# One megakernel, new queues: the output norm's sums of squares on ScalarE, setup work off VectorE, one silu for two more chunks

## The chip, the cores and the metric

One core of one Trainium2 chip runs the whole program in one launch. The metric is the device time of that launch in microseconds.

## The reference

Two layers, each a recurrent mixer followed by a mixture of experts, on an input of 16 x 16 x 8 positions with 64 channels (fp32):

```python
# mixer, both layers; H, W, B, D = 16, 16, 8, 64
feat = ln(x) @ in_w + in_b            # 64 -> 192
inp, og, fg = split(feat, 3)
inp, og, lam = silu(inp), sigmoid(og), sigmoid(fg)
# outer product by head (2x2), scans forward and back along H and along W
inp_o = (1 - lam)[..., None] * inp[..., None, :]
state = bidir_scan_h(inp_o, lam) + bidir_scan_w(inp_o, lam)
out = einsum('...hde,...hd->...he', state, og).reshape(H, W, B, D)
out = (out - out.mean(-1)) * rsqrt(out.var(-1) + 1e-5) * gamma + beta
x = x + out @ out_w + out_b
# layer 0 experts: 16, hidden 128, top 2, softmax over the two
h = silu(ln(x) @ w1[e]) * (ln(x) @ w2[e]);  x = x + sum_e gate_e * (h @ w3[e])
# layer 1 experts: 8, hidden 256, top 2
h = gelu(ln(x) @ W1[e] + b1[e]);            x = x + sum_e gate_e * (h @ W2[e] + b2[e])
```

Both feed-forward parts compute every expert for every position and weigh the results by gates that are zero outside the top two.

## The kernel before, in words

The batch is cut into four groups of two images (512 positions). A **unit** is one layer of one group: units 0 to 3 are layer 0, units 4 to 7 are layer 1. The mixer works in **chunks**: chunks 0 and 1 are the two images of unit 0 (256 positions each), chunks 2 to 8 are units 1 to 7. An expert of one unit is a **step**: steps 0 to 63 are layer 0, steps 64 to 95 layer 1; two steps make a **pair**, whose products down are weighed and added together.

Nothing is looped: the table `ORDER` lists by hand, for each engine, the stages in the order in which it runs them, and `BANK_USES` lists who uses which of the eight PSUM banks in turn. Every engine works strictly through its list; a stage that waits holds back all that is listed behind it. Stages are linked by semaphores.

One chunk of the mixer goes, with the names of the lists (number = chunk): `a_stats` (VectorE, mean and variance of the rows, and `a_parts`, `a_norm`: the norm, split into two parts), `a_turn` (TensorE transposes), `a_z` (ScalarE copy), `p_f`, `p_i`, `p_o` (TensorE, projections with `in_hi` and `in_lo`), `t_f`, `t_i`, `t_o` (ScalarE, tanh and silu), `lam_fw/rw/fh/rh` (ScalarE, decay factors), `add_w` (VectorE), `add_h` (ScalarE), `fwd_*`, `rev_*` (VectorE scans), `sum_*`, `gate_o` (VectorE), `heads` (TensorE, with `heads_w`: the first half of each result is the head sum, the second the output product), `b_stats` (statistics of the first half), `b_rstd` (GpSimd), `b_res` (VectorE, residual), `e_stats`, `e_norm`, `e_parts`, `e_turn`, `e_z` (second norm, transposed into `tok_z`).

The experts: `up_a`, `up_b` (TensorE, two matmuls each), `act` (ScalarE, silu, layer 0; gelu in layer 1), `hid` (VectorE product, layer 0) or `act_b` (ScalarE gelu of the second half, layer 1), `down` (TensorE), `weigh` (VectorE), `add` (GpSimd). The gates: `logits` (TensorE), `top` (VectorE), `t_m` (ScalarE), `gates` (GpSimd), `g_turn` (TensorE), `g_copy` (ScalarE), then a write to DRAM and a broadcast back by SyncE's queue into `gates_b`. `x_turn` and `x_res` add the experts' sum to the rows; layer 1 of a group needs them.

Expert weights of layer 0 are split into two parts as well: `round` (ScalarE) makes the high part of a pair, `split` (GpSimd) the low part, and `up_a` of the pair waits for it. Pairs 0 and 1 wait for the first block of up weights, pairs 2 to 7 for the second.

Setup before: VectorE rounds and subtracts the gate weights (`gate_w0`), spreads the input weights over both parities and splits them (`in_w`), and widens the biases and vectors (`b_wide0`, `v_wide0`), which TensorE turns (`b_turn0`, `v_turn0`). Small products (`products0`) and their copies (`biases0`) give folded biases.

For chunks in `BY_TANH` the silu of `t_i` is made of a tanh and an Identity on ScalarE and one more product on VectorE (`value`); for the others it is one Silu:

```python
if not two_branches(c):
    nc.scalar.activation(bank, bank, ACT.Silu, bias=column(l, I_B)).then_inc(s_value, 1)
    return
```

The output norm before reads mean and variance on VectorE:

```python
for t in range(count):
    last = nc.vector.bn_stats(stats[n][:, k, t, :], ...)
link(last)
for t in range(count):
    last = nc.vector.bn_aggr(moments[n][:, k, t, :], stats[n][:, k, t, :])
```

Of the kernel before, what the change touches and what calls it, by code (L numbers as in the profile page):

```python
# [1410 lines left out]
```

## Time and profile before

| | |
|---|---|
| median of 3 runs | 256.01 us (255.82 to 257.69) |
| profiled execution | 255.79 us |
| span of its instructions | 253.9 us |
| PE busy | 210.3 us, 83% |
| DVE busy | 195.0 us, 77% |
| ACT busy | 165.8 us, 65% |
| POOL busy | 129.9 us, 51% |

The profiled execution is 1.9 us longer than its span. PE is TensorE, DVE is VectorE, ACT is ScalarE, POOL is GpSimd. Shares are averages over stages that differ: the first 51 us hold the setup and the first chunks of the mixer, then experts and mixer chunks of both layers are interleaved. A duration in the rows is that of one instruction from start to end; instructions of one engine overlap, so the distance between starts is what one costs in a row of many.

### The profile page before, as it was taken

To read this page: it belongs to the slowest core of one execution; us is meant where nothing else is said; L and a number is where in the kernel's file an instruction comes from. 1 tells how busy PE (TensorE), PEld (TensorE's weight loads), DVE (VectorE), ACT (ScalarE), POOL (GpSimd) and SP (SyncE) were. 2 spreads that over 40 slices of the span, in tenths; PEclk is the share of its full clock that TensorE was granted. 3 is DMA by queue.
4 is the path that set the end of the run, shared out by engine and by line. 5 is a ranking of instruction groups with operands and counts; after the bars stand their busy time and mean duration, and the time that the engine had idled before them with its cause. 6 is when DMAs were issued, how large, how long until landed. Compare 5 with 4: busy or idle time off the path is not lost. (4 is left out here: it accounts for less than half of the span.)

```text
span 253.9 us, 3842 instructions
## 1 busy us (share of the span) xinstructions
PE 210.3 (83%) x940; PEld 127.1 (50%) x940; DVE 195.0 (77%) x621; ACT 165.8 (65%) x323; POOL 129.9 (51%) x206
## 2 busy tenths in 40 slices
PE   0052985777979899999798999899999999999992
PEld 0042764543535555656364655555565654744640
DVE  0378499989989999959699999979996199634233
ACT  2039589948644473869578443599959998485560
POOL 3115389850875495875344541785728632453212
PEclk9999999799999999999999999999999999999998
DMA  1199700026940194009629300000800704400450
GB/s 37 53 211 185 134 1 1 0 82 137 202 83 0 44 209 88 0 8 218 114 66 203 69 0 3 1 3 3 165 1 5 167 0 108 83 0 1 88 121 21
DMA packets 18544, 18.50 MB, mean 73 GB/s; under 512 B 5350, under 2 KB 12284, under 8 KB 18524
## 3 DMA queue, kind: packets, MB, share of 16 engines
q1 hardware_dynamic: 18524, 18.28, 35.3%
q8 instruction: 7, 0.11, 0.2%
q14 instruction: 13, 0.11, 0.2%
HBM read 17.56 MB, written 0.72 MB: 72 GB/s over the span
## 5 line engine op out<-in xcount | busy, mean ns | idle before, releaser
L1232 PE MATMUL SPARE<-tok_z,up_hi 128*128 128x512 f32 x192 | 81.3, 424 | 5.0 <-ACT silu_h L837 1.6
L1233 PE MATMUL SPARE<-tok_z,up_lo 128*128 128x512 f32 x192 | 75.4, 393 | 0.0
L538 POOL TENSOR_TENSOR total<-total,weighted 128x512 f32<-128x512 f32 x39 | 50.1, 1285 | 45.2 <-DVE weighted L1158 25.9
L1350 PE MATMUL SPARE<-hidden,down 128*64 128x512 f32 x256 | 60.9, 602 | 2.3 <-DVE hidden L1137 1.2
L837 ACT ACTIVATE silu_h<-SPARE 128x512 f32<-128x512 f32 x64 | 37.8, 597 | 28.6 <-PE SPARE L1233 28.6
L1232 PEld LDWEIGHTS SPARE<-tok_z,up_hi 128*128 128x128 f32 x192 | 36.0, 188 | 34.0 <-issue 10.9
L1137 DVE TENSOR_TENSOR hidden<-silu_h,SPARE 128x512 f32<-128x512 f32 x64 | 42.0, 674 | 1.5 <-PE SPARE L1233 0.9
L1233 PEld LDWEIGHTS SPARE<-tok_z,up_lo 128*128 128x128 f32 x192 | 36.2, 188 | 5.3
L1350 PEld LDWEIGHTS SPARE<-hidden,down 128*64 128x64 f32 x256 | 16.6, 136 | 30.3 <-issue 23.7
L843 ACT ACTIVATE hidden<-SPARE,expert_bias 128x512 f32<-128x512 f32 x32 | 21.8, 683 | 10.5 <-PE SPARE L1350 9.9
L1236 PE MATMUL SPARE<-ident,parts_a 128*128 128x128 f32 x32 | 7.0, 352 | 20.5 <-DVE parts_a L1012 15.4
L850 ACT ACTIVATE hidden<-SPARE,expert_bias 128x512 f32<-128x512 f32 x32 | 21.9, 684 | 2.4 <-PE SPARE L1233 2.4
L1158 DVE TENSOR_TENSOR weighted<-SPARE,gates_b 128x512 f32<-128x512 f32 x28 | 18.6, 681 | 2.5 <-DMA gates_b<-gates_dram 1.2
L681 POOL TENSOR_TENSOR up_lo<-up_raw,up_hi 128x512 fp32r<-128x512 f32 x12 | 15.2, 1277 | 9.1 <-ACT up_hi L731 9.1
L1232 PE MATMUL SPARE<-conv_z,in_hi 128*128 128x512 f32 (+1 forms) x27 | 14.0, 520 | 4.2 <-issue 3.0
L1236 PEld LDWEIGHTS SPARE<-ident,parts_a 128*128 128x128 f32 x32 | 4.8, 179 | 22.3 <-issue 20.4
L1160 DVE SCALAR_TENSOR_TENSOR weighted<-SPARE,expert_bias,gates_b 128x512 f32<-128x512 f32 x12 | 9.0, 746 | 8.0 <-PE SPARE L1350 8.0
L757 ACT ACTIVATE conv_z<-SPARE 128x512 fp32r<-128x512 f32 (+1 forms) x9 | 4.8, 538 | 14.5 <-PE SPARE L1236 14.5
L661 POOL TENSOR_SCALAR spread_a<-moments_a 128x4 f32<-128x4 f32 (+1 forms) x9 | 2.3, 252 | 21.9 <-DVE moments_a L992 21.7
L1286 PE MATMUL SPARE<-heads_w,gated 128*128 128x128 f32 x64 | 10.1, 302 | 3.4 <-issue 2.9
L1233 PE MATMUL SPARE<-conv_z,in_lo 128*128 128x512 f32 (+1 forms) x27 | 12.7, 471 | 0.0
L741 ACT ACTIVATE norm_e<-rows,shift_e,rstd_e 128x64 f32<-128x64 f32 x28 | 10.1, 437 | 3.7 <-POOL shift_e L666 3.6
(133 smaller groups left out, 366.4 us busy)
## 6 DMA issues: line engine op xcount, KB each, us to landing
gates_b<-gates_dram SPq DMA_DIRECT2D x6, 1024.0 KB, 9.9
gates_b<-gates_dram SPq DMA_DIRECT2D x8, 512.0 KB, 6.0
up_raw<-in_L_ffn_w_dram SPq DMA_DIRECT2D x4, 384.0 KB, 7.9
gates_b<-gates_dram SPq DMA_DIRECT2D x2, 768.0 KB, 11.3
up_raw<-in_L_ffn_W_dram SPq DMA_DIRECT2D x2, 512.0 KB, 6.0
up_raw<-in_L_ffn_w_dram SPq DMA_DIRECT2D x4, 128.0 KB, 3.7
down<-in_L_ffn_w_dram SPq DMA_DIRECT2D x1, 512.0 KB, 10.4
down<-in_L_ffn_W_dram SPq DMA_DIRECT2D x1, 512.0 KB, 5.1
```

Source lines behind the costliest of these rows:

```text
L538: nc_engine.tensor_tensor(t, t, weighted[:, q % WEIGHED_RING, :], ALU.add).then_inc(s_sum, 1)
L681: nc.gpsimd.tensor_tensor(up_lo[l][:, e, :, :], up_raw[:, e, :, :], up_hi[l][:, e, :, :].bitcast(fp32), ALU.subtract).then_inc(s_split, 1)
L741: last = nc.scalar.activation(norm[n][:, k, t, :], tile[:, t // HALF, t % HALF, :], ACT.Identity, bias=shift[n][:, k, t:t + 1], scale=rstd ...
L837: nc.scalar.activation(silu_h[:, at % SILU_RING, :], spare("up_a", n), ACT.Silu).then_inc(s_silu_h, 1)
L843: nc.scalar.activation(hidden[:, hidden_slot(n) % RING, :], spare("up_a", n), ACT.Gelu, bias=expert_bias[:, 2 * i:2 * i + 1]).then_inc(s_h ...
L850: nc.scalar.activation(hidden[:, hidden_slot(n, 1) % RING, :], spare("up_b", n), ACT.Gelu, bias=expert_bias[:, 2 * i + 1:2 * i + 2]).then_ ...
L1137: nc.vector.tensor_tensor(hidden[:, hidden_slot(n) % RING, :], silu_h[:, STEP_AT[n] % SILU_RING, :], spare("up_b", n), ALU.mult).then_inc( ...
L1158: nc.vector.tensor_tensor(dst, spare("down", q), g, ALU.mult).then_inc(s_pm, 1)
L1232: nc.tensor.matmul(dst, hi, z, start=True, stop=False)
L1233: return nc.tensor.matmul(dst, lo, z, start=False, stop=True)
L1236: return nc.tensor.transpose(dst, src, ident[0:k, 0:k])
L1350: last = nc.tensor.matmul(spare("down", q)[k * D:(k + 1) * D, :], w, hidden[:, at, :], start=(j == 0), stop=(j == chunks - 1))
```

## The change

**Output norm.** The head matrix `heads_w` gets -1/64 added, so that the first half of the `heads` result is the head sum less its mean. `b_stats` moves from VectorE (4 BN_STATS and 4 BN_AGGR per chunk of four tiles) to ScalarE: one Square per tile with an accumulated sum, written in place in PSUM. GpSimd makes the variance from the sums in the same number of instructions as before.

**Setup.** `gate_w0` leaves VectorE: ScalarE rounds (`gate_hi0`), GpSimd subtracts (`gate_w0`). The input weights are rounded by ScalarE in six activations (`in_hi`) and subtracted by VectorE in six instructions (`in_w`), without `in_wide`. `b_wide0` and `v_wide0` move to ScalarE.

**Silu.** `BY_TANH` shrinks from chunks 5 to 8 to chunks 7 and 8: chunks 5 and 6 lose the tanh on ScalarE and the product on VectorE.

**Orders.** All lists of `ORDER` and `BANK_USES` are new. A path by which GpSimd could make hidden products is added, but `BY_POOL` is empty, so that none of it runs.

```diff
-BY_TANH = tuple(c for c in range(len(CHUNKS)) if UNITS_AT[CHUNKS[c][0]] not in ((0, 0), (0, 1), (0, 2), (0, 3)))
+BY_TANH = (7, 8)
+
+BY_POOL = ()
...
-        "gate_w0 a_stats0 a_stats1 in_w0 a_parts0 b_wide0 v_wide0 b_cols0 a_parts1 add_w0 a_stats2 a_stats3 "
+        "a_stats0 a_stats1 a_parts0 a_parts1 in_w0 b_cols0 v_cols0 add_w0 out_w0 fwd_w0 fwd_h0 rev_w0 rev_h0 "
...
-                nc.gpsimd.tensor_copy(heads_w[:, l, 0, :], over_d[:, :]).then_inc(s_over, 1)
+                nc.gpsimd.tensor_scalar(heads_w[:, l, 0, :], over_d[:, :], -1.0 / D, None, ALU.add).then_inc(s_over, 1)
...
+                if n == "b":
+                    link(nc.gpsimd.tensor_scalar(spread[n][:, k, t], squares[:, k, t], 1.0 / D, eps, ALU.mult, ALU.add))
...
+            def in_high(l):
+                act.wait_ge(s_in[l], 32)
+                for parity in range(2):
+                    for which in (FORGET, OUTPUT, INPUT):
+                        last = copy(of_parity(in_hi[:, l, which, :], which, parity), in_part(l, which))
+                last.then_inc(s_in_hi, 1)
...
+            def head_squares(c):
+
+                act.wait_ge(s_heads, c + 1)
+                if c >= 2:
+                    act.wait_ge(s_rstd["b"], c - 1)
+                heads = heads_of(c)[0]
+                for t in range(chunk_tiles(c)):
+                    last = nc.scalar.activation(heads[:, t, :], heads[:, t, :], ACT.Square,
+                                                accum_out=squares[:, c % 2, t:t + 1])
+                last.then_inc(s_stats["b"], 1)
...
-                link(last)
-                link(nc.vector.tensor_copy(in_hi[:, l, :, :], fog[:, :, :]))
-                nc.vector.tensor_tensor(in_lo[:, l, :, :], fog[:, :, :], in_hi[:, l, :, :].bitcast(fp32),
-                                        ALU.subtract).then_inc(s_conv_w, 1)
+                dve.wait_ge(s_in_hi, l + 1)
+                for parity in range(2):
+                    for which in (FORGET, OUTPUT, INPUT):
+                        last = nc.vector.tensor_tensor(
+                            of_parity(in_lo[:, l, which, :], which, parity), in_part(l, which),
+                            of_parity(in_hi[:, l, which, :].bitcast(fp32), which, parity), ALU.subtract)
+                last.then_inc(s_conv_w, 1)
```

**VectorE at the start of the program, before.** `stats_a` and `norm_a` belong to the first norm, `gate_parts` to the gate weights:

```order
L970 CAST gate_parts<-gate_raw 128x16 [waits conv_weights_loaded0]
L970 CAST gate_parts<-gate_raw 128x8 [waits conv_weights_loaded1]
L974 TENSOR_TENSOR gate_parts<-gate_raw,gate_parts 128x16 [waits vector_chain]
L974 TENSOR_TENSOR gate_parts<-gate_raw,gate_parts 128x8
L988 BN_STATS stats_a<-rows 128x6 [waits rows_loaded_first]
L988 BN_STATS stats_a<-rows 128x6
L992 BN_AGGR moments_a<-stats_a 128x2 [waits vector_chain]
```

**VectorE at the start, now:**

```order
L1071 BN_STATS stats_a<-rows 128x6 [waits rows_loaded_first]
L1071 BN_STATS stats_a<-rows 128x6
L1074 BN_AGGR moments_a<-stats_a 128x2 [waits vector_chain]
L1074 BN_AGGR moments_a<-stats_a 128x2
L1081 TENSOR_TENSOR norm_a<-rows,moments_a 128x128 [waits moments_ready_a]
L1071 BN_STATS stats_a<-rows 128x6 [waits rows_loaded_first]
L1071 BN_STATS stats_a<-rows 128x6
L1074 BN_AGGR moments_a<-stats_a 128x2 [waits vector_chain]
L1074 BN_AGGR moments_a<-stats_a 128x2
```

The four instructions on the gate weights, which wait for the loads of both layers' small weights, no longer stand ahead of the first statistics of the rows.

**ScalarE at the start of the program, before.** `conv_z` is `a_z`; `tanh_f` is `t_f`:

```order
L854 ACTIVATE warm<-minus_half 128x4 [waits constants_ready]
L757 ACTIVATE conv_z<-SPARE 128x256 [waits norm_turned_a]
L766 ACTIVATE tanh_f<-SPARE,half_bias 128x256 [waits columns_ready,forget_projected]
L774 ACTIVATE SPARE<-SPARE,columns 128x256 [waits input_projected]
L787 ACTIVATE tanh_o<-SPARE,half_bias 128x256 [waits output_projected]
L801 ACTIVATE lam_rh<-tanh_f 128x15x16 [waits pads_zeroed,tanh_f_ready]
L801 ACTIVATE lam_fh<-tanh_f 128x15x16 [waits pads_zeroed,tanh_f_ready]
```

**ScalarE at the start, now:**

```order
L963 ACTIVATE warm<-minus_half 128x4 [waits constants_ready]
L785 ACTIVATE in_hi<-in_raw 128x64 [waits in_weights_loaded0]
L785 ACTIVATE in_hi<-in_raw 128x64
L785 ACTIVATE in_hi<-in_raw 128x32x2
L785 ACTIVATE in_hi<-in_raw 128x64 x2
L785 ACTIVATE in_hi<-in_raw 128x32x2
L785 ACTIVATE wide<-vectors 2x64 [waits in_biases_loaded]
L785 ACTIVATE wide<-vectors 2x64
L785 ACTIVATE wide<-vectors 2x32x2
L785 ACTIVATE wide<-vectors 2x64 x2
L785 ACTIVATE wide<-vectors 2x32x2
L848 ACTIVATE conv_z<-SPARE 128x256 [waits norm_turned_a]
```

Twelve small activations on the input weights and biases now stand ahead of the first `conv_z`.

**ScalarE around the last steps of layer 0 and the first of layer 1, before** (silu_h is `act` of layer 0, line 843 and 850 are `act` and `act_b` of layer 1; `tanh_f`, `lam_*`, `tanh_i` here are chunk 7):

```order
L766 ACTIVATE tanh_f<-SPARE,half_bias 128x512 [waits lambdas_ready_rw,lambdas_ready_fw,lambdas_ready_fh,row_inputs_ready,lambdas_ready_rh,columns_ready,forget_projected]
L837 ACTIVATE silu_h<-SPARE 128x512 [waits hidden_ready0,up_first_bank]
L801 ACTIVATE lam_rw<-tanh_f 128x32x15 [waits row_scans_done,pads_zeroed,tanh_f_ready]
L801 ACTIVATE lam_rh<-tanh_f 128x2x15x16 [waits column_scans_done,pads_zeroed,tanh_f_ready]
L801 ACTIVATE lam_fw<-tanh_f 128x32x15 [waits row_scan_forward_done,pads_zeroed,tanh_f_ready]
L822 ACTIVATE tanh_m<-margin 128x4 [waits gates_ready,margin_ready]
L801 ACTIVATE lam_fh<-tanh_f 128x2x15x16 [waits column_scan_forward_done,pads_zeroed,tanh_f_ready]
L837 ACTIVATE silu_h<-SPARE 128x512 [waits hidden_ready0,up_first_bank] x2
L778 ACTIVATE tanh_i<-SPARE,half_bias 128x512 [waits input_products_ready,input_projected]
L781 ACTIVATE SPARE<-SPARE,columns 128x512 [waits tanh_i_ready]
L829 ACTIVATE gates_t<-SPARE 8x512 [waits gates_sent1,gates_turned]
L843 ACT_TABLE_LOAD [waits pair_down_done,biases_ready]
```

**The same place now** (lines 945 and 959 are the gelus):

```order
L945 ACT_TABLE_LOAD [waits pair_down_done,biases_ready]
L945 ACTIVATE hidden<-SPARE,expert_bias 128x512 [waits up_first_bank]
L959 ACTIVATE hidden<-SPARE,expert_bias 128x512 [waits up_second_bank,pair_down_done]
L945 ACTIVATE hidden<-SPARE,expert_bias 128x512 [waits pair_down_done,up_first_bank]
L959 ACTIVATE hidden<-SPARE,expert_bias 128x512 [waits up_second_bank,pair_down_done]
L917 ACTIVATE tok_z<-SPARE 128x512 [waits logits_product,up_second_bank,norm_turned_e]
L945 ACTIVATE hidden<-SPARE,expert_bias 128x512 [waits pair_down_done,up_first_bank]
L959 ACTIVATE hidden<-SPARE,expert_bias 128x512 [waits up_second_bank,pair_down_done]
L945 ACTIVATE hidden<-SPARE,expert_bias 128x512 [waits pair_down_done,up_first_bank]
L857 ACTIVATE tanh_f<-SPARE,half_bias 128x512 [waits lambdas_ready_rw,lambdas_ready_fw,lambdas_ready_fh,row_inputs_ready,lambdas_ready_rh,columns_ready,forget_projected]
L869 ACTIVATE tanh_i<-SPARE,half_bias 128x512 [waits input_projected]
L872 ACTIVATE SPARE<-SPARE,columns 128x512 [waits tanh_i_ready]
```

Chunk 7's `t_f` and `t_i` (and its `lam_*` behind them) now stand behind the first seven gelus of layer 1, where they stood ahead of them.

## Rows read from the trace of the kernel before

**Rows 1.** Busy time by stretch (windows: start:end, length, busy and count of each engine).

```profile
11.00:31.20 20.20, 10.45 (x43) 8.54 (x43) 14.80 (x69) 11.68 (x31) 8.25 (x15) 1.00 0.98 181
31.20:54.20 23.00, 17.07 (x61) 12.70 (x60) 21.38 (x85) 19.66 (x37) 19.53 (x29) 0.93 0.01 2
54.20:173.90 119.70, 109.25 (x490) 64.72 (x491) 110.46 (x312) 75.00 (x145) 66.42 (x93) 1.00 0.39 81
173.90:248.30 74.40, 72.94 (x345) 40.70 (x343) 45.58 (x152) 57.98 (x109) 32.53 (x52) 1.00 0.30 63
```

**Rows 2.** Timeline, the last 10 us (start, duration, engine, line, operation, count, idle before).

```profile
244.63 3.65 PE L1350 MATMUL SPARE<-hidden,down 128*64 128x512 f32 x16
244.93 0.75 DVE L1160 SCALAR_TENSOR_TENSOR total<-SPARE,expert_bias,gates_b 128x512 f32<-128x512 f32 x1 [5.39 <-DMA gates_b<-gates_dram]
```

**Rows 3.** Waits from 54.2 to 173.9 us (who waited for whom: us, times, longest).

```profile
ACT silu_h L837 <- PE SPARE L1233: 27.8, 35, 3.4
```

**Rows 4.** Timeline of VectorE, the first steps.

```profile
10.66 0.17 DVE L970 CAST gate_parts<-gate_raw 128x8 fp32r<-128x8 f32 x1 [1.80 <-DMA gate_raw<-in_L_ffn_Wg_dram]
...
11.03 0.34 DVE L988 BATCH_NORM_STATS2 stats_a<-rows 128x6 f32<-128x64 f32 x2
...
12.77 0.19 DVE L929 COPY in_wide<-in_raw 128x64 f32<-128x64 f32 x1
...
14.96 0.29 DVE L1012 TENSOR_TENSOR parts_a<-norm_a,parts_a 128x128 f32<-128x128 f32 x1
...
18.60 0.60 DVE L988 BATCH_NORM_STATS2 stats_a<-rows 128x6 f32<-128x64 f32 x4
```

**Rows 5.** Timeline of TensorE: first projection, the first experts.

```profile
16.53 0.58 PE L1232 MATMUL SPARE<-conv_z,in_hi 128*128 128x256 f32 x1
...
32.16 0.63 PE L1232 MATMUL SPARE<-conv_z,in_hi 128*128 128x512 f32 x1
32.59 0.63 PE L1233 MATMUL SPARE<-conv_z,in_lo 128*128 128x512 f32 x1
...
51.10 0.47 PE L1232 MATMUL SPARE<-tok_z,up_hi 128*128 128x512 f32 x1 [0.52 <-issue]
...
52.56 0.40 PE L1232 MATMUL SPARE<-tok_z,up_hi 128*128 128x512 f32 x1
52.79 0.39 PE L1233 MATMUL SPARE<-tok_z,up_lo 128*128 128x512 f32 x1
```

**Rows 6.** Loads: SyncE's timeline, landing times by line, and the up weights' tile.

```profile
0.72 0.44 SPq L545 DMA_DIRECT2D rows<-in_x_dram  x1
...
10.28 0.40 SPq L545 DMA_DIRECT2D rows<-in_x_dram  x1
...
rows<-in_x_dram SPq DMA_DIRECT2D x1, 384.0 KB, 3.5
rows<-in_x_dram SPq DMA_DIRECT2D x1, 128.0 KB, 2.2
...
L555 SPq DMA_DIRECT2D up_raw<-in_L_ffn_w_dram x8: 616/636/1868, 10.7 to 15.5; - x8
...
DMA to landing us min/median/max: 3.7/4.8/10.2
```

**Rows 7.** Timelines of VectorE and ScalarE between the biases and the first expert.

```profile
31.25 0.29 DVE L957 COPY conv_bias<-SPARE 128x128 f32<-128x128 f32 x1 [3.25 <-PE SPARE L1236]
...
54.21 0.68 DVE L1137 TENSOR_TENSOR hidden<-silu_h,SPARE 128x512 f32<-128x512 f32 x1
...
38.06 1.40 ACT L741 ACTIVATE norm_a<-rows,shift_a,rstd_a 128x64 f32<-128x64 f32 x4
...
51.85 0.60 ACT L837 ACTIVATE silu_h<-SPARE 128x512 f32<-128x512 f32 x1 [0.85 <-PE SPARE L1233]
```

**Rows 8.** Busy time of the output norm's statistics alone (windows of one tile).

```profile
54.20:173.90 119.70, 3.96 (x32) 1.00 0.39 81
```

**Rows 9.** Groups by line (count, busy us, mean ns, idle before).

```profile
L1023 DVE SCALAR_TENSOR_TENSOR SPARE<-tanh_i,SPARE 128x512 f32<-128x512 f32 x4 | 2.8, 688 | 0.2 <-ACT SPARE L781 0.2
```

More of the change, by code:

```diff
@@ L106, in step_layer, with by_pool, hidden_by, made_before @@
     return layer(STEP_UNIT[n])
+def by_pool(n):
+    return step_layer(n) == 0 and n - steps_before(STEP_UNIT[n]) in BY_POOL
+def hidden_by(n):
+    return ("act_b" if step_layer(n) else "product" if by_pool(n) else "hid", n)
+def made_before(n):
+    return sum(by_pool(m) == by_pool(n) for m in LAYER_STEPS[0] if m <= n)
 def hidden_slot(n, j=0):
@@ L261, in drained_by @@
     if kind == "up_b":
-        return ("act_b" if step_layer(i) else "hid", i)
+        return ("copy", i) if by_pool(i) else hidden_by(i)
     return (DRAINED_BY[kind], i)
@@ L392, in metaformer, with in_part, of_parity @@
         GATE_AT, EXPERT_AT, HEADS_AT = LAYERS * D, LAYERS * (D + 16), LAYERS * (D + 16) + 32
+        def in_part(l, which):
+            first = {FORGET: 2, INPUT: 0, OUTPUT: 1}[which] * D
+            return in_raw[:, l, first:first + D] if which != INPUT else in_raw[:, l, first:first + D].rearrange("p (h e) -> p h e", e=2)
+        def of_parity(t, which, parity):
+            return t[:, parity:P:2] if which != INPUT else t.rearrange("p (h d e) -> p h d e", d=2, e=2)[:, :, parity, :]
         def places(c):
@@ L528, in wait_bank @@
                     wait_hidden(eng, v)
+                elif reader == "copy":
+                    eng.wait_ge(s_copy, made_before(v))
                 else:
@@ L675, in low_parts, with gate_weights @@
                                         ALU.subtract).then_inc(s_low[n], 1)
+            def gate_weights():
+                pool.wait_ge(s_gate_hi, 1)
+                for l in range(LAYERS):
+                    pool.wait_ge(s_small[l], 16 * 3)
+                    e = EXPERTS[l]
+                    last = nc.gpsimd.tensor_tensor(gate_parts[:, l, 1, 0:e], gate_raw[:, l, 0:e],
+                                                   gate_parts[:, l, 0, 0:e].bitcast(fp32), ALU.subtract)
+                last.then_inc(s_gate_w, 1)
             def split_up(pair):
@@ L708, in _ @@
                 elif kind == "b_rstd":
-                    make_rstd("b", u, SCALE[layer(unit(u))] * SCALE[layer(unit(u))] * EPS_T)
+                    make_rstd("b", u, SCALE[two_branches(u)] * SCALE[two_branches(u)] * EPS_T)
                 elif kind == "e_rstd":
@@ L726, in _, with copy, widen_in_biases, widen_vectors @@
         def _(act):
+            def copy(dst, src):
+                return nc.scalar.activation(dst, src, ACT.Copy)
+            def widen_in_biases():
+                act.wait_ge(s_in_b, 16 * LAYERS)
+                for e in range(2):
+                    copy(wide[:, F_B, e:P:2], vectors[:, 2 * D:3 * D])
+                    copy(wide[:, O_B, e:P:2], vectors[:, D:2 * D])
+                    last = copy(
+                        wide[:, I_B, :].rearrange("p (h d e) -> p h d e", d=2, e=2)[:, :, e, :],
+                        vectors[:, 0:D].rearrange("p (h e) -> p h e", e=2))
+                last.then_inc(s_wide, 1)
+            def widen_vectors():
+                act.wait_ge(s_vectors, 16 * 4 * LAYERS)
+                both = wide[:, GAMMA:BETA + 1, :].rearrange("p w (k d) -> p w k d", k=2)
+                once = vectors[:, 3 * D:5 * D].rearrange("p (w d) -> p w d", d=D)
+                for k in range(2):
+                    last = copy(both[:, :, k, :], once)
+                last.then_inc(s_wide, 1)
+            def in_high(l):
[4 more added lines that the diff above has]
+                last.then_inc(s_in_hi, 1)
+            def gate_high():
+                for l in range(LAYERS):
+                    act.wait_ge(s_small[l], 16 * 3)
+                    last = copy(gate_parts[:, l, 0, 0:EXPERTS[l]], gate_raw[:, l, 0:EXPERTS[l]])
+                last.then_inc(s_gate_hi, 1)
             def round_up(pair):
@@ L871, in _ @@
                     column_inputs(u)
+                elif kind == "b_stats":
+                    head_squares(u)
                 elif kind == "e_z":
@@ L881, in _ @@
                     second_half(u)
+                elif kind == "in_hi":
+                    in_high(u)
+                elif kind == "b_wide":
+                    widen_in_biases()
+                elif kind == "v_wide":
+                    widen_vectors()
+                elif kind == "gate_hi":
+                    gate_high()
+                elif kind == "copy":
+                    copy_second(u)
                 elif kind == "round":
@@ L908, in in_biases @@
                 nc.vector.tensor_scalar(half_bias[:, :, :], turned_biases, 0.5, None, ALU.mult).then_inc(s_columns, 1)
-            def widen_vectors():
-                dve.wait_ge(s_vectors, 16 * 4 * LAYERS)
-                both = wide[:, GAMMA:BETA + 1, :].rearrange("p w (k d) -> p w k d", k=2)
-                once = vectors[:, 3 * D:5 * D].rearrange("p (w d) -> p w d", d=D)
-                for k in range(2):
-                    last = nc.vector.tensor_copy(both[:, :, k, :], once)
-                last.then_inc(s_wide, 1)
             def vectors_ready():
@@ L993, in make_moments @@
                 last.then_inc(s_stats[n], 1)
-                if n != "b" and not by_scalar(n, c):
+                if not by_scalar(n, c):
                     dve.wait_ge(s_stats[n], c + 1)
```

89 lines of the change are left out of this document (36 added, 53 removed), and 166 rows, old and new, of tables (BANK_USES, ORDER).

## Prediction

> **What bounds the kernel now.** I read the stretches first, then the start, then the waits inside the long middle. [rows 1] cut the program in four. From 11 to 31 us (setup and the first two images) no engine is full: VectorE 14.8 of 20.2 us. From 31.2 to 54.2 us VectorE is nearly full (21.4 of 23.0) and ScalarE close behind (19.7). From 54.2 to 173.9 us, layer 0's 64 experts with mixer chunks between them, VectorE (110.5 of 119.7) and TensorE (109.3) share the bound, while ScalarE (75.0) mostly waits for TensorE, 27.8 us in 35 waits at its silu alone [rows 3]. From 173.9 to 248.3 us, layer 1, TensorE has 72.9 of 74.4 us and is the bound alone. The last products down end 3.65 us after 244.63; the first weighing of unit 7, which waits 5.39 us for the gates' broadcast, runs meanwhile at 244.93 [rows 2], so the stream of TensorE and not the gates sets the end, by little. Only what makes that stream start earlier or wait less counts.
>
> **The start.** VectorE's first work on the rows begins at 11.03 us, because the second rounding of the gate weights stands ahead and waits for its load until 10.66 us [rows 4]. The rows are there far earlier: issued at 0.72 us, landed 2.2 us later [rows 6], so 2.9 us. With the gate weights off VectorE's list its statistics begin 8.1 us earlier. By the distances in [rows 4] the first `a_parts` ends at 15.25, 4.2 us after 11.03, of which `in_w0` took some 1.6 (from 12.77); it would end near 5.6 us, the second one 0.9 to 1.3 us later, near 6.9. Six subtractions then remain, which the trace does not show in this shape; at 0.1 to 0.22 us each, 0.6 to 1.3, they end near 7.9. On ScalarE twelve activations of 64 elements stand ahead of the first `a_z`. The nearest row is the norm's: four of 128x64 take 1.40 us together [rows 7], 0.33 apart, with two pointer operands that a plain copy lacks; the other end is 0.1 apart, as the short ones go. So 1.2 to 4 us from about 4 us on; I take 3.5, so 7.5 to 8. The first projection stood at 16.53 [rows 5] and I expect it at about 8.5: 8 us earlier. Cover for ScalarE's copies is that VectorE needs until 7.9 us anyway.
>
> The Trainium skill ("ScalarE: Activation LUTs", section "What ACT_TABLE_LOAD costs") gives an ACTIVATE with immediate scale and bias as 186 ns + 0.833 ns per element, 93 ns more for each pointer operand, neighbours overlapping by 93 ns. For 64 elements that is 239 ns, 146 ns apart, so 1.8 us for the twelve where I take 3.5; by it the first projection would come some 0.5 us earlier yet, since VectorE is then last, and the sum below would be 244.0.
>
> What is late next? Loads that do not move. The rest of the rows is issued at 10.28 and lands 3.5 us later, at 13.8; chunks 2 and 3 take their statistics at 18.60 before [rows 4, 6], so they can come 4.8 us earlier and not 8. The up weights of pairs 0 and 1 land at about 16.5 (fourth of eight issues between 10.7 and 15.5 us, plus 3.7 us), those of pairs 2 to 7 at 15.5 + 10.2 = 25.7 us [rows 6]. In the new list of ScalarE `round0` and `round1` stand ahead of `add_h1` and `a_norm2`, `round2` ahead of `lam_fw2`; these waits, up to 1 us each, hold back all behind them. The 3.3 us in which VectorE waited for the small products before `biases0` at 31.25 are gone, because other work now stands there. Walking VectorE's new list from its first scan at about 12.3 us (behind `out_w0`, which needs the load of 10.66): four scans of 256 positions 2.4, eight statistics 1.9, `add_w1` and two sums 1.0, two scans and a sum 1.5, so `biases0` at 19.1 at the earliest, 12 us before 31.25.
>
> From `biases0` to the first `hid` VectorE needed 23.0 us before (31.25 to 54.21) [rows 7], nearly without a gap; its new list up to `hid0` holds the same 23 us by the same distances (three scans more, less `b_stats` and `b_res` of chunk 2), and ScalarE's new list from `a_norm2` at about 18 us to `act0` adds up to 23.4 us, two Squares runs and seven `round` among them. Without any wait that is 41.4 us for `act0`, against 51.85. Before, ScalarE had 3.3 us of gaps in that stretch of 23 [rows 1]; with as many, `act0` comes at 44.5 and `hid0` at about 46: 8 us earlier, with a range of 5 to 10.5. **Start: -8.0.**
>
> **Layer 0.** VectorE loses between 54.2 and 173.9 us: the statistics of the output norm of four chunks, 3.96 us [rows 8]; two of the four products by tanh (688 ns, 0.6 apart) [rows 9], 1.2; in `in_w1` some 0.5; and about 1.6 of scans that are now done before `hid0`, while `e_stats6` with 1.0 us comes in. That is 6.3 of 110.5 us. TensorE's share is untouched, and it waited only 10.4 us of the 119.7. So the gain lies between 1 us (TensorE was the one that held) and 6.3. VectorE is a little fuller; I take 4.0. ScalarE gets the Squares of these chunks: not in the trace; the nearest row, of the same shape, gives 1.4 us a chunk [rows 7], plain spacing 0.6, and if each had a second instruction of 0.2 us behind it, 2.5. I take 1.4: 5.6 us, less 1.3 for the silus, on an engine with 44.7 us free. It does cost latency where a Square is queued behind other work, and the wait for `b_res` starts there; I count that inside the range. GpSimd's added gate subtraction and its constant are in its first idle 11 us: nothing. `BY_POOL` is empty: nothing. **Layer 0: -4.0.**
>
> **Layer 1.** TensorE's own 72.9 us stay. ScalarE had 58.0 of 74.4 [rows 1]. Chunk 7's `t_f`, `t_i` and `lam_*` move into this stretch (4.7), one `e_norm` and some copies out of it (2.9), two runs of Squares come in (2.8): 62.6. It fits as a mean, yet the first three units of layer 1, where a mixer chunk and two gelus a step meet, are denser. **Layer 1: +0.5**, from -1 to +3.
>
> **Sum.** Span 253.9 - 8.0 - 4.0 + 0.5 = 242.4; with the 1.9 us outside the span 244.3, and the median lies 0.2 above the profiled execution: 244.5 us.
>
> **Rivals.** *ScalarE's queue eats the head start* (0.20). For it: ScalarE had 19.7 of 23.0 us from 31.2 on, and now gets `b_stats0` to `b_stats2` and sits on two loads. If Squares cost 2.5 us a chunk and every load wait is paid, the start gives 5 and layer 0, where `b_res` waits longer, 1.5: 253.9 - 6.5 + 1 + 2.1 = 250.5. Against it: VectorE is the fuller in the same stretch. The Trainium skill (same page, "Rules for kernel authors") says to keep adds and multiplies on VectorE and not on ScalarE; by that rule the Squares and copies lose, and the result would be this rival's. [rows 1] speak against: the engine that gives the work away is the full one.
>
> *VectorE was the bound all along* (0.10): the start gives 10 and layer 0 its whole 6.3 us, layer 1 loses nothing: 253.9 - 16.3 + 2.1 = 239.7.
>
> *TensorE starts its stream at its low level* (0.03), the one that ends slower. Up matmuls go 0.23 us apart at 52.56, those of the projections at 32.16 0.43 apart [rows 5], that is the level of 2.4 GHz and of 1.2. Before, the stream began behind a run of projections. If now the first steps come thinly between waits and TensorE stays at the low level, a step of six matmuls costs 1.2 us more; ten steps eat the 11.5 us gained, and twelve give 259. Against it: VectorE's list still sets a run of products ahead of `up_a0`.
>
> *It does little* (0.04): a gain at the start is lost where the order puts a stage ahead of its turn again and again, 254 to 257.
>
> **How the numbers follow.** Forecast 0.63, 241.5 to 248.5 as its own range. The range to hold 8 in 10 takes in the quick rival and most of the slow queue: 239.5 to 250.5. A measurement can tell about 1% here, 2.6 us. Faster by over 1% (under 253.4): forecast, quick rival and queue, 0.93. Within 1%: 0.04. Slower: 0.03.
>
> **What the changed profile would show.** Right: statistics of the rows at 3 us; first projection at 8 to 9; `biases0` at 19 to 21; first silu near 44.5; 64 steps of layer 0 in 115 to 118 us from `hid0`; layer 1 within 1 us of 74.4. Wrong: if ScalarE's activations of 64 elements with the sum take over 0.45 us apart; if `act0` is later than 47 us; if the step from `hid0` to layer 1 still takes 119 us, so that TensorE held it; or if ScalarE is full in layer 1 and TensorE waits there for gelus.

## The result, and the profile after

The changed kernel takes 246.3 us, the median of four runs (243.8 to 249.6), against 255.9 for the kernel before in the same session: a ratio of 0.959 (95% interval 0.949 to 0.969). Run again beside the first experiments it took 245.2 us against 255.3, ratio 0.9625 (0.958 to 0.967). The forecast was 244.5 us. The first profiled execution of the changed kernel was a disturbed one, so the rows below are of the second.

The span is 243.4 us, 10.5 shorter than before. These rows of the timelines (start, duration, engine, line, operation, idle before) answer to [rows 4, 5, 7 and 2]:

```profile
3.12 0.35 DVE L1071 BATCH_NORM_STATS2 stats_a<-rows 128x6 f32<-128x64 f32 x2 [3.12 <-DMA rows<-in_x_dram]
...
4.04 0.99 ACT L785 ACTIVATE in_hi<-in_raw 128x64 fp32r<-128x64 f32 x6 [1.77 <-DMA in_raw<-in_L_conv_in_w_dram]
...
8.22 0.58 PE L1305 MATMUL SPARE<-conv_z,in_hi 128*128 128x256 f32 x1
...
16.52 1.15 ACT L822 ACTIVATE up_hi<-up_raw 128x512 fp32r<-128x512 f32 x2 [1.72 <-DMA up_raw<-in_L_ffn_w_dram]
...
19.47 0.28 DVE L1054 COPY conv_bias<-SPARE 128x128 f32<-128x128 f32 x1
...
42.47 0.63 PE L1305 MATMUL SPARE<-tok_z,up_hi 128*128 128x512 f32 x1
...
46.27 0.69 ACT L878 ACTIVATE tanh_o<-SPARE,half_bias 128x512 f32<-128x512 f32 x1 [2.18 <-DVE gated L1165]
...
46.28 0.98 PE L1359 MATMUL SPARE<-heads_w,gated 128*128 128x128 f32 x3 [2.76 <-issue]
...
47.38 0.59 ACT L939 ACTIVATE silu_h<-SPARE 128x512 f32<-128x512 f32 x1
...
49.45 0.67 DVE L1219 TENSOR_TENSOR hidden<-silu_h,SPARE 128x512 f32<-128x512 f32 x1
...
233.89 3.65 PE L1424 MATMUL SPARE<-hidden,down 128*64 128x512 f32 x16
```

The statistics begin 7.9 us earlier, the first projection 8.3, the biases 11.8, the first up product 8.6. But the first silu comes only 4.5 us earlier and the first `hid` 4.8: the head start is gone by half within 5 us. The rest comes later: from the first `hid` to layer 1's first up product (163.02) it is 113.6 us instead of 119.7.

Cut at the first up product and at those of steps 16 and 64, the windows (start:end, length, then busy and count of TensorE, its weight loads, VectorE, ScalarE, GpSimd, then TensorE's granted clock, DMA) show where. Before, with layer 1 in [rows 1]:

```profile
0.00:51.10 51.10, 24.52 (x88) 19.01 (x89) 34.27 (x140) 31.05 (x66) 27.55 (x59) 0.97 0.41 78
51.10:83.18 32.08, 26.91 (x113) 14.65 (x113) 29.90 (x86) 18.04 (x35) 16.95 (x24) 1.00 0.45 99
83.18:173.90 90.72, 85.34 (x393) 52.29 (x393) 82.95 (x243) 58.75 (x115) 52.08 (x73) 1.00 0.35 72
```

After:

```profile
0.00:42.47 42.47, 23.73 (x85) 18.52 (x86) 31.18 (x111) 32.91 (x87) 25.56 (x58) 0.84 0.51 93
42.47:77.63 35.16, 30.93 (x133) 19.23 (x132) 34.88 (x90) 25.52 (x75) 22.04 (x33) 0.86 0.45 91
77.63:163.02 85.39, 81.84 (x376) 49.72 (x373) 76.68 (x211) 54.50 (x123) 48.71 (x71) 1.00 0.43 88
163.02:237.50 74.48, 74.25 (x349) 41.25 (x347) 42.06 (x126) 61.57 (x125) 32.15 (x49) 1.00 0.22 49
```

Take TensorE's busy time from each length: it idled 26.6, 5.2, 5.4 and 1.5 us before, 18.7, 4.2, 3.6 and 0.2 after. That is 11.8 us less idling against 1.0 us more busy time (part of it at a lower granted clock, 0.84 and 0.86 in the first two windows), 10.8 us to the end of its stream. TensorE is the fullest engine in steps 16 to 64 (96% busy) and in layer 1 (99.7%); VectorE is full in the first 16 steps alone (34.9 of 35.2).

The new lists move work into those 16 steps. On TensorE 133 matmul records stand there instead of 113: `heads2`, `heads4`, `e_turn3` and `g_turn1` came in (24 matmuls), `logits0` went out (4). The next 48 steps have 376 instead of 393, since `heads4`, `e_turn3` and `g_turn1` left them for the first 16 and `p_f7` and `p_i7` for layer 1. VectorE has 34.9 us of work there instead of 29.9, and 76.7 instead of 83.0 in the next 48.

### The profile page after: what moved, and what is told of

It is laid out like the page before. It is cut to its first block, busy times and chain, and to the rows that moved or that the text cites. A ratio compares the mean times of both kernels' runs of the same rounds, so it can differ in the third digit from the quotient of the medians.

```text
span 247.7 us, 3864 instructions
## 1 busy us (share of the span) xinstructions
PE 213.3 (86%) x940; PEld 131.2 (53%) x940; DVE 187.2 (76%) x539; ACT 174.4 (70%) x407; POOL 129.7 (52%) x208
## 4 chain that ended last, share of the span: by engine, by line
PE 51%; DMA 11%; issue 9%; POOL 9%; DVE 7%; ACT 6%; SPq 4%; POOLq 1%; ACTq 0%; DVEq 0%
PE SPARE L1305 15%; PE SPARE L1424 14%; PE SPARE L1306 13%; DMA gates_b<-gates_dram 8%; PE SPARE L1309 5%; POOL total L572 4%; PE SPARE L1359 2%; POOL rstd_a L699 2%; DMA rows<-in_x_dram 2%; DMA gates_dram<-gates_t 2%; PE SPARE L1370 1%; DVE hidden L1219 1%; SPq L596 1%; SPq L605 1%; SPq L640 1%
## 5 line engine op out<-in xcount | busy, mean ns | idle before, releaser
L1305 PE MATMUL SPARE<-tok_z,up_hi 128*128 128x512 f32 x192 | 83.1, 433 | 0.9 <-ACT silu_h L939 0.6
L1306 PE MATMUL SPARE<-tok_z,up_lo 128*128 128x512 f32 x192 | 77.4, 403 | 0.0
L1305 PEld LDWEIGHTS SPARE<-tok_z,up_hi 128*128 128x128 f32 x192 | 37.2, 194 | 23.5 <-issue 10.0
L1306 PEld LDWEIGHTS SPARE<-tok_z,up_lo 128*128 128x128 f32 x192 | 37.3, 194 | 6.3
L959 ACT ACTIVATE hidden<-SPARE,expert_bias 128x512 f32<-128x512 f32 x32 | 22.3, 696 | 5.8 <-PE SPARE L1306 5.6
L945 ACT ACTIVATE hidden<-SPARE,expert_bias 128x512 f32<-128x512 f32 x32 | 22.2, 693 | 3.5 <-PE SPARE L1424 3.3
L1309 PEld LDWEIGHTS SPARE<-ident,parts_a 128*128 128x128 f32 x32 | 4.6, 178 | 18.7 <-issue 14.4
L1306 PE MATMUL SPARE<-conv_z,in_lo 128*128 128x512 f32 (+1 forms) x27 | 13.2, 489 | 0.0
L1359 PE MATMUL SPARE<-heads_w,gated 128*128 128x128 f32 x64 | 10.6, 315 | 2.9 <-issue 2.8
L1359 PEld LDWEIGHTS SPARE<-heads_w,gated 128*128 128x128 f32 x64 | 10.0, 227 | 5.3 <-issue 4.8
L1120 DVE TENSOR_TENSOR_SCAN fwd_w<-lam_fw,SPARE 128x512 f32<-128x512 f32 (+1 forms) x9 | 9.9, 1095 | 2.8 <-ACT SPARE L908 2.2
L698 POOL TENSOR_SCALAR spread_a<-moments_a 128x4 f32<-128x4 f32 (+1 forms) x9 | 2.2, 242 | 18.7 <-DVE moments_a L1074 18.4
## 6 DMA issues: line engine op xcount, KB each, us to landing
gates_b<-gates_dram SPq DMA_DIRECT2D x2, 768.0 KB, 11.8
```

The costliest lines, as they stand in the source:

```text
L945: nc.scalar.activation(hidden[:, hidden_slot(n) % RING, :], spare("up_a", n), ACT.Gelu, bias=expert_bias[:, 2 * i:2 * i + 1]).then_inc(s_h ...
L959: nc.scalar.activation(hidden[:, hidden_slot(n, 1) % RING, :], spare("up_b", n), ACT.Gelu, bias=expert_bias[:, 2 * i + 1:2 * i + 2]).then_ ...
L1305: nc.tensor.matmul(dst, hi, z, start=True, stop=False)
L1306: return nc.tensor.matmul(dst, lo, z, start=False, stop=True)
L1309: return nc.tensor.transpose(dst, src, ident[0:k, 0:k])
L1359: last = nc.tensor.matmul(spare("heads", c)[:, t * P:(t + 1) * P], states[:, t * P:(t + 1) * P], weights, start=True, stop=True)
```

## The experiments

Each ratio is against the kernel before, run in the same session; its median lay between 255.3 and 255.8 us in these sessions, so half a microsecond between two medians of different sessions says nothing. The times of single stages are of one profiled execution each. "Kernel 1" is the kernel of experiment 1. In the diffs a name is an entry of the order lists. "Step 16" is the start of its first up product.

**1. The gate weights alone.** The kernel before with one entry moved.

```diff
 "DVE":
-gate_w0 a_stats0 a_stats1 in_w0 ... a_stats3 fwd_w0
+a_stats0 a_stats1 in_w0 ... a_stats3 gate_w0 fwd_w0
```

> The kernel before with one edit: gate_w0 stands in VectorE's list just ahead of fwd_w0 and no longer first. If the head start is the gate weights' doing alone, the rows' statistics start at 3 us and the first projection comes at about 9; since the old order then runs into the load of the remaining rows (13.8 us) and ScalarE's list is unchanged, my theory expects 3 to 5 us of the 8 to survive at the end: 251 to 253 us. Rival (the old order cannot use an earlier start, because the later loads of the up weights and the small products bind it): 255 to 256.

Measured: 249.8 us, 0.980 (0.977 to 0.983), better than the 251 to 253 expected. One moved entry gives 5.4 of the 10 us. Its first up product is at 46.08, its first silu at 46.82 and its first `hid` at 49.22, where the changed kernel has 42.47, 47.38 and 49.45. Step 16 is at 77.26, as early as the changed kernel's 77.63; steps 16 to 64 take 90.5 us and layer 1 74.3, as before. So the new lists' earlier first up product does not bring step 16 forward; what it can have bought is room for the work moved into these steps.

**2. The head start taken away.** The changed kernel, VectorE held.

```diff
+            for l in range(LAYERS):
+                dve.wait_ge(s_small[l], 16 * 3)
             for kind, u in order["DVE"]:
```

> The changed kernel with one wait more: VectorE waits for both gate weight loads (landed at 10.7 us) ahead of its first statistics, so the start is as late as before while all else is new. Theory (most of the gain is the start): 6 to 8 us are lost, 251 to 254 us. Rival (the start was hidden behind later loads, and the gain is the relief of VectorE in layer 0 and the order): under 3 us are lost, 246 to 248 us.

Measured: 250.4 us, 0.985 (0.978 to 0.992), 5.2 us slower than the changed kernel: between the two theories, nearer to the first. VectorE begins at 10.65, step 16 comes at 81.79 (4.2 later), and steps 16 to 64 take 85.5 us: the gain there does not hang on the start.

**3. The output norm's statistics back on VectorE,** in the new lists, up to three places ahead of each `b_res`.

```diff
-"ACT": ... b_stats0 t_f2 ...
+"DVE": ... b_stats0 (and 1 to 8) ahead of b_res
-                    link(nc.gpsimd.tensor_scalar(spread[n][:, k, t], squares[:, k, t], 1.0 / D, eps, ALU.mult, ALU.add))
+                    link(nc.gpsimd.tensor_scalar(spread[n][:, k, t], moments[n][:, k, t, 1], eps, None, ALU.add))
```

> The changed kernel with b_stats back on VectorE (BN_STATS and BN_AGGR of the centred head sums, put two or three stages ahead of b_res), ScalarE's Squares gone, all else new. Theory (VectorE holds layer 0 as much as TensorE): 8.2 us more work on VectorE costs 3 to 5 us, 248 to 250 us. Rival (TensorE holds layer 0, so that the Squares bought nothing): within 1.5 us of the changed kernel. A second rival, that ScalarE is the engine in want: it gets faster by 1 to 2 us.

Measured: 252.4 us, 0.988 (0.982 to 0.994), 7.2 slower than the changed kernel: more than any of the theories. The profiled execution was the longest of the four, 254.4 us. Its windows from step 16 and from step 64:

```profile
80.11:167.59 87.48, 83.56 (x375) 51.13 (x373) 78.89 (x235) 53.32 (x107) 48.83 (x71) 0.98 0.42 86
167.59:246.40 78.81, 76.36 (x349) 41.92 (x347) 43.67 (x142) 60.03 (x109) 32.05 (x48) 0.98 0.21 46
```

To step 16 it loses 2.5 us. Steps 16 to 64 are 2.1 us longer than the changed kernel's 85.39, but most of that is TensorE's clock and not the norm. The granted clock was 0.50 from 101 to 104 us, and 0.98 over the window. The kernel of experiment 10, whose lists in these steps are the changed kernel's own, had such a stretch too in its profile:

```profile
76.76:163.38 86.62, 83.38 (x376) 51.02 (x373) 76.81 (x211) 54.90 (x123) 48.70 (x71) 0.98 0.43 87
```

Against this one some 0.9 us are left for the statistics, so 3.4 in layer 0, within the theory's 3 to 5. The other 4.3 fall in layer 1 and are my placement more than the norm: `b_stats8` stands right ahead of `b_res8`, VectorE waits 1.5 us for rstd there, and TensorE 1.9 us for gates that come late, as GpSimd has them behind that rstd. Right behind this wait the granted clock is 0.50 for some 3.5 us, which costs 1.6 more.

**4. The Squares alone, in the old lists.** Kernel 1 with centred head weights and ScalarE's sums of squares.

```diff
 "DVE":
-... gate_o1 b_stats0 fwd_w2 b_stats1 ... (and 2 to 8)
 "ACT":
+lam_fw2 b_stats0 ... add_h2 b_stats1 ... e_z0 e_z1 b_stats2 act0 ... act6 b_stats3 ...
```

> The kernel before with gate_w0 moved (which ran at 249.8 us) and, on top, the output norm alone in its new form: centred head weights, sums of squares by ScalarE put into ScalarE's old list where the heads come, b_stats struck from VectorE's list, nothing else moved. If the statistics were worth their time on VectorE (3.96 us in layer 0 and some in the start), 246 to 247 us. If the Squares take from ScalarE's list what they give VectorE's, as they wait for the heads ahead of silus, 249 to 251 us, and then the new orders, and not the norm, earned the second half of the gain.

Measured: 259.6 us, 1.015 (1.008 to 1.023): 9.8 us slower than kernel 1, outside both theories. VectorE's timeline:

```profile
49.78 0.86 DVE L1074 SCALAR_TENSOR_TENSOR rows<-SPARE,rstd_b,rows 128x64 f32<-128x64 f32 x4 [4.49 <-POOL rstd_b L632]
...
70.42 0.86 DVE L1074 SCALAR_TENSOR_TENSOR rows<-SPARE,rstd_b,rows 128x64 f32<-128x64 f32 x4 [1.76 <-POOL rstd_b L632]
```

The heads of chunk 2 were there at 43.5; ScalarE's Squares of them ran at 47.4, behind its other work, and VectorE stood still. By step 16 (84.51) 7.3 us are lost, in layer 1 another 2.2. TensorE's clock has a part in the first: between the first up product and step 16 its granted clock was 0.86, where kernel 1 had 1.00, and the same 112 matmul records were busy for 29.6 us instead of 26.3. How much of the loss is the clock's was not tried.

**5. The same with better places.**

```diff
 "ACT":
+... a_z4 b_stats2 t_o3 ... act70 b_stats7 t_m5 ...
 "DVE":
+... top0 b_res2 hid0 ... weigh1 b_res3 hid8 ... x_res5 b_res8 e_stats8 ...
```

> The output norm alone on the kernel before with gate_w0 moved, as in the run of 259.6 us, with five moves: the Squares of chunk 2 six places earlier and of chunk 7 three places earlier on ScalarE, the residuals of chunks 2, 3 and 8 some places later on VectorE (with them the statistics of chunk 8). In that run VectorE waited 4.5, 1.8, 2.3 and 3.0 us for rstd of chunks 2, 3, 7 and 8. If those waits were the loss, and not the Squares' own time on ScalarE, 247 to 251 us. If the Squares' time on ScalarE is the loss, 256 us or more.

Measured: 258.2 us, 1.010 (1.006 to 1.013), 8.4 us slower than kernel 1: the second theory's time, though not by the Squares' own time (0.95 us a chunk). VectorE's waits for rstd are down to 1.6 us in all, the time is not: ScalarE now waits 0.7 us for heads ahead of its token copies, the first up product comes at 50.09 instead of 46.08, and the residuals hold the heads' bank longer (TensorE waits 1.86 us for it at 54.85). The granted clock is 0.86 here too up to step 16, which comes at 84.51 again. The window from step 16 to 64:

```profile
84.51:175.25 90.74, 85.41 (x394) 52.22 (x392) 80.30 (x219) 61.36 (x139) 51.84 (x73) 1.00 0.36 72
```

VectorE has 2.3 us less to do than in kernel 1 (82.6), and the stretch is no shorter.

**6. The silu for chunks 5 and 6 alone, in the old lists.** Kernel 1 with two products fewer on VectorE.

```diff
-BY_TANH = tuple(c for c in range(len(CHUNKS)) if UNITS_AT[CHUNKS[c][0]] not in ((0, 0), (0, 1), (0, 2), (0, 3)))
+BY_TANH = (7, 8)
 "DVE":
-... value5 ... value6 ...
```

> The kernel before with gate_w0 moved (249.8 us) and, on top, chunks 5 and 6 in the silu form: value5 and value6 struck from VectorE's list, nothing else moved. Given back to the changed kernel, the tanh form made steps 16 to 64 2.0 us longer (87.4 against 85.4 us). If VectorE's work is what those steps wait for in the old order too, steps 16 to 64 take 88 to 89 us instead of 90.5, and the kernel 247.5 to 248.8 us. If in the old order something else sets the pace there (taking statistics off VectorE left its 90.5 us as they were), within 0.6 us of 249.8.

Measured: 251.0 us, 0.978 (0.972 to 0.983), no gain over kernel 1 (0.980). Steps 16 to 64 took 90.4 us, with VectorE busy for 81.9 us instead of 82.6. Twice, VectorE's work was taken out of the old order's middle, and twice nothing came of it.

**7. The tanh form given back** to chunks 5 and 6 in the changed kernel.

```diff
-BY_TANH = (7, 8)
+BY_TANH = (5, 6, 7, 8)
 "DVE":
+... value5 add_w5 ... value6 add_w6 ...
```

> The changed kernel with the tanh form for chunks 5 and 6 again (value5 and value6 back on VectorE, 688 ns apiece by four each, and a shorter product on ScalarE). If VectorE bounds layer 0's stream as before, 1 to 2 us longer than the changed kernel: 246.2 to 247.2 us. If VectorE has slack there, within 0.5 us of 245.2.

Measured: 247.2 us, 0.968 (0.963 to 0.974); the expectation held, though the interval touches the changed kernel's. The window from step 16 to 64:

```profile
78.19:165.56 87.37, 82.75 (x376) 49.24 (x373) 78.11 (x213) 55.67 (x124) 48.80 (x71) 1.00 0.43 86
```

It is 2.0 us longer than the changed kernel's, at the same granted clock, 1.1 of it TensorE idling. So in the new order these products do count, for more than the 1.4 us that VectorE is busy longer.

**8. The early stage in other orders.** In one kernel `gate_o2` ahead of `top0` and six splits late, in another `gate_o2` alone.

```diff
 "DVE":
-... sum_wh2 top0 gate_o2 fwd_w3 ...
+... sum_wh2 gate_o2 top0 fwd_w3 ...
 "POOL":
-... e_rstd1 split2 split3 split4 split5 split6 split7 b_rstd2 gates0 b_rstd3 ...
+... e_rstd1 b_rstd2 gates0 split2 split3 split4 split5 split6 split7 b_rstd3 ...
```

> The changed kernel with gate_o2 ahead of top0 on VectorE and GpSimd's splits 2 to 7 behind gates0. In the profile heads2 waited for gate_o2, which stood behind the top-two work, and three small VectorE instructions took 1.0 to 1.3 us beside GpSimd's splits. If the first stage's order costs what it shows, up_b0 comes some 2.5 us earlier and the whole is 1.5 to 3 us shorter than the changed kernel: 242.5 to 243.7 us. The rival: late splits hold back the first ups (each pair waits for its split) and the time is the same or up to 2 us longer.

Measured: 253.3 us, 0.992 (0.989 to 0.995), 7 to 8 us slower than the changed kernel and outside both theories. Step 8 did come 2.1 us earlier (57.88), then step 16 came at 84.58, 7 late. Timelines of ScalarE, GpSimd and SyncE's queue:

```profile
50.12 7.50 POOL L704 TENSOR_TENSOR up_lo<-up_raw,up_hi 128x512 fp32r<-128x512 f32 x6
...
57.64 1.30 SPq L568 DMA_DIRECT2D up_raw<-in_L_ffn_W_dram  x2
...
64.88 0.63 ACT L798 ACTIVATE up_hi<-up_raw 128x512 fp32r<-128x512 f32 x1 [7.61 <-DMA up_raw<-in_L_ffn_W_dram]
```

A split is what frees a buffer of raw weights; the next load was issued only at 57.64 (48.86 in the changed kernel), and ScalarE's rounding waited 7.6 us for it with the silus queued behind.

> The changed kernel with gate_o2 ahead of top0 on VectorE, and GpSimd's splits left where they were. In the run that also put the splits late, step 8 came 2 us earlier, and then the loads behind the late splits cost 7 us. If only VectorE's amount of work counts, a move of work within its list gives at most 1 us: 244.2 to 245.7 us. If the early heads2 fill VectorE's and TensorE's gap of 2.8 us, 1.5 to 2.5 us shorter than the changed kernel: 242.7 to 243.7 us.

Measured: 246.1 us, 0.960 (0.956 to 0.965): no gain. The heads of chunk 2 stand at 42.76 instead of 46.28, TensorE's gap of 2.8 us is gone, and step 16 comes at 77.38 (77.63).

**9. TensorE kept busy.** Matmuls of 384 columns whose results are overwritten, ahead of four waits.

```diff
+WARM = {("a", 3): 4, ("a", 4): 6, ("e", 0): 6, ("h", 2): 8}
+            def warm(dst, n):
+                for _ in range(n):
+                    nc.tensor.matmul(dst[:, 0:3 * P], in_hi[:, 0, 0, :], ...)
```

> The changed kernel with 24 matmuls of 384 columns added on TensorE whose results are overwritten: 4 and 6 ahead of the turns of chunks 3 and 4, 6 ahead of the first token turn, 8 ahead of heads2, all in its waits between 31 and 47 us. There the granted clock was 0.50 and matmuls of 512 columns came 0.43 us apart until about 50 us. If TensorE's idling there is why the first ups run at the low level, they come 0.23 apart from the first on; if that level also costs time, the whole is 1 to 3 us shorter. My theory is that VectorE and ScalarE bound the stream, so that the time is within 1 us of the changed kernel's, or up to 1 us longer from the added work. If the level is set by something other than the engine's own activity, the spacing stays 0.43.

Measured: 246.4 us, 0.966 (0.959 to 0.973). Two rows of each kernel's windows, first the changed kernel, then this one:

```profile
31.00:46.00 15.00, 7.90 (x23) 4.98 (x21) 13.35 (x37) 11.60 (x23) 10.44 (x11) 0.50 0.00 1
46.00:60.00 14.00, 12.79 (x50) 9.33 (x50) 13.97 (x30) 11.98 (x40) 5.79 (x11) 0.77 0.46 96
```

```profile
31.00:46.00 15.00, 9.21 (x49) 7.03 (x48) 14.52 (x39) 13.32 (x31) 11.20 (x13) 1.00 0.00 1
46.00:60.00 14.00, 11.51 (x42) 8.18 (x44) 13.09 (x32) 10.66 (x32) 5.74 (x12) 0.76 0.57 118
```

Up to 46 us the granted clock goes from 0.50 (1.2 GHz) to 1.00 (2.4 GHz). Behind the filling it falls all the same, in the waits of the first steps, and from 46 to 60 us it is no higher than before. The first up product comes at 40.41 instead of 42.47, the first `hid` at 46.24 instead of 49.45 and step 14 at 69.1 instead of 71.3. Then VectorE has to wait for a transfer, the broadcast of the first gates:

```profile
70.86 1.29 DVE L1241 TENSOR_TENSOR weighted<-SPARE,gates_b 128x512 f32<-128x512 f32 x2 [1.33 <-DMA gates_b<-gates_dram]
```

Step 16 comes at 76.85 instead of 77.63, and the span is 1.0 us shorter in this one profile. The timed runs show no gain. So the first steps did come quicker in this profile, and most of that was lost at the gates. What the low level costs there is not settled by this run, as it came back from 48 to 55 us.

**10. Both together,** `gate_o2` early and the filling, to see whether they beat the changed kernel.

```diff
 "DVE":
+... sum_wh2 gate_o2 top0 fwd_w3 ...
+WARM = {("a", 3): 4, ("a", 4): 6, ("e", 0): 6, ("h", 2): 8}
```

> The changed kernel with gate_o2 ahead of top0 and the 24 matmuls of filling on TensorE between 31 and 47 us. The filling alone gave the first ups at 0.23 us apart and a span 1.0 us shorter in one profile. If the early TensorE finds its work waiting once heads2 come early, 242 to 243.5 us, below the one of gate_o2 alone by 0.5 to 1 us; if VectorE takes all of the slack, the same as with gate_o2 alone within 0.4 us.

Measured: 245.7 us, 0.961 (0.957 to 0.964), 0.5 us from `gate_o2` alone and from the changed kernel, which is within the noise. Nothing beat the changed kernel. With `gate_o2` early, with the filling and with both, step 16 comes at 77.38, 76.85 and 76.76 instead of 77.63, though the first `hid` came 1.8 to 3.2 us earlier. VectorE, busy for 34.9 of 35.2 us in the changed kernel, leaves little to win there; that it alone sets the end of that stage is not shown, as the gates' broadcast stood in the way in experiment 9.

## Why the prediction was right, and where its terms were not

The mechanism was right in its two halves, a head start and a shorter layer 0. The total came right by luck, from two terms that were each off, in opposite directions: the start is that of the slow rival (5 us), layer 0 that of the quick one (6.3).

- **Start, -8.0: mis-sized.** It measured -4.8, outside the stated 5 to 10.5, and `act0` at 47.4 is past the 47 us that the prediction had set as a sign of being wrong. The early milestones came as worked out (3.12, 8.22, `biases0` at 19.5); the twelve activations took 1.9 us (4.04 to 5.90) where 3.5 was taken, but VectorE was last, until 7.95, as foreseen. The term that failed is the stretch from `biases0` to the first `hid`: 26.9 us was allowed (19.1 to 46), and it took 30.0. The windows of that stretch, after and before:

```profile
19.47:49.45 29.98, 18.63 (x60) 14.00 (x61) 25.88 (x70) 23.97 (x58) 20.77 (x29) 0.65 0.42 66
31.25:54.21 22.96, 17.02 (x60) 12.65 (x60) 21.39 (x85) 19.66 (x37) 19.53 (x29) 0.93 0.01 2
```

  VectorE's new list was priced at 23 us, and it was busy for 25.9: three small instructions took some 0.9 us more each (last section), 2.8 in all. It also idled 4.1 us, above all for ScalarE and for the gates' logits, where 3.3 had been allowed. TensorE idled 2.76 us and ScalarE 2.18 us for `gate_o2`, which stands behind `top0`, but VectorE ran without a gap meanwhile, and experiment 8 shows that taking this idling away brought nothing. Experiment 1 shows that with the old lists step 16 comes as early from a first up product at 46.08 as here from 42.47. The head start is what gives half of the gain (experiments 1 and 2: 5.4 and 5.2 us), where two thirds had been foreseen.
- **Layer 0, -4.0: it measured -6.1,** near the upper bound of 6.3, and 113.6 us from `hid0` are below the 115 to 118 expected. VectorE was busy 5.8 us less there. Yet the reason behind the bound was wrong in part. VectorE's work taken out does nothing in the old lists (experiments 5 and 6); put back in the new ones it costs some 0.9 us of steps 16 to 64 for the statistics and 2.0 for the two products (3 and 7). TensorE's busy time in these steps fell by 3.5 us, as work of its own left them, and its idling by 1.8; the new lists have a part in both. I had taken "new orders" as a carrier of the other edits, and they are an edit of their own. Of the 5.3 us that steps 16 to 64 became shorter, the two edits account for some 2.9 if they add up, which no run tried; how the other 2.4 divide among the lists was not tried either.
- **The Squares:** four take 0.95 us a chunk, in eight instructions, inside the bounds of 0.6 to 2.5 and under the 1.4 taken. Their place can cost far more than their time: 9.8 us in the old lists.
- **Layer 1, +0.5: it measured +0.1.** TensorE is at 99.7% and ScalarE at 61.6 of 74.5 us (62.6 foreseen). Behind the stream of TensorE the end takes 0.3 us more than before, which the sum left out.
- **ScalarE's queue eats the head start** did not come, but experiment 4 is this rival in full size, with the old lists: whoever gives the Squares to ScalarE without a new order gets a slower kernel than before. The Trainium skill's rule ("ScalarE: Activation LUTs", "Rules for kernel authors") to keep adds and multiplies on VectorE would make the Squares lose: they did in the old lists, and not in the new ones, where taking them back to VectorE cost 7.2 us, part of it by its placement.
- **VectorE was the bound all along:** not all along, as the old lists show; its time for layer 0 came all the same.
- **TensorE starts its stream at its low level:** it did, with up matmuls 0.43 us apart until about 52 us, through three steps and not twelve. What that cost is open: experiment 9 took the low level from these steps, and it came back in the next ones.

## What to carry to other kernels

Add up where the pacing engine idles, stage by stage, before crediting work taken off its neighbour: 2.3 us off VectorE bought nothing in the old lists. Compare a stage of two profiles only with the granted clock beside it: a fall of the clock for three microseconds looked like a cost of the norm. Work moved onto an engine with an in-order queue must be priced with its place, and with what its buffer or result releases (a late split delayed a load by far more than it took). A single early entry that waits for a load is the first thing to look for: moving it gave half of the gain of the whole change.
